# Three layer-norm statistics of every chunk, taken from VectorE and summed by ScalarE with its accumulator, in a Mamba block with a routed expert layer

## What is computed

```python
def _L0_attn_ref(x, ...):
    x = x + _mamba(_ln(x, n1_g, n1_b), ...)
    normed = _ln(x, n2_g, n2_b)
    gate, val = jnp.split(normed @ ffg_w.T + ffg_b, 2, axis=-1)
    return x + jax.nn.silu(gate) * val @ ffp_w.T + ffp_b
...
x = x + _L0_attn_ref(_layernorm(x, axis=-1), ...)   # the first norm, then _ln inside
x = x + _L0_ffn_ref(_layernorm(x, axis=-1), ...)    # top 2 of 8 experts, softmax weights
```

## Time and profile before

| | |
|---|---|
| runs | 896.98, 898.70, 903.21 us; median 898.7 us |
| the profiled execution | 898.42 us, of which the span of the engines is 896.5 us |
| VectorE | 726.3 us busy, 81% |
| TensorE | 666.5 us busy, 74% |
| GpSimd | 573.2 us busy, 64% |
| ScalarE | 504.6 us busy, 56% |
| scan phase | from about 45 us to 746 us |
| tail (expert tiles and the last chunk's output side) | 746 us to the end |

### The profile page before, as it was taken

How to read it: one execution, slowest core, us unless ns; L and a number is a source line. 1 busy time by engine, 2 the same in 40 slices (tenths; PEclk the granted TensorE clock), 3 DMA queues, 4 the chain that set the end, 5 groups by cost and what they waited for, 6 DMA issues and landing times. The chain is left out here.

```text
span 896.5 us, 13066 instructions
## 1 busy us (share of the span) xinstructions
PE 666.5 (74%) x3706; PEld 481.6 (54%) x3706; DVE 726.3 (81%) x1128; ACT 504.6 (56%) x1092; POOL 573.2 (64%) x488
## 2 busy tenths in 40 slices
PE   4358578678768886797788768877884877898963
PEld 2134245445335534774477446744673556798963
DVE  1378779989998999979998999999999865474363
ACT  2547676766766576556756575557553663443421
POOL 1095556566856895789768985888669934345332
PEclk9679699889879977998799988988797889999997
DMA  6833133213312336542654255434642423457794
GB/s 179 248 113 114 47 94 118 79 65 108 119 48 90 106 100 185 152 127 86 186 162 118 90 171 155 125 106 132 173 150 80 129 63 99 135 160 216 204 311 130
DMA packets 95450, 118.24 MB, mean 132 GB/s; under 512 B 11351, under 2 KB 63395, under 8 KB 95363
## 3 DMA queue, kind: packets, MB, share of 16 engines
q1 hardware_dynamic: 90835, 108.02, 41.3%
q0 software_dynamic: 4544, 9.38, 2.9%
HBM read 105.37 MB, written 16.34 MB: 136 GB/s over the span
## 5 line engine op out<-in xcount | busy, mean ns | idle before, releaser
L695 POOL TENSOR_TENSOR inflow<-du,b_wide 128x1024 f32<-128x1024 f32 x128 | 316.2, 2473 | 170.6 <-DVE product L960 109.4
L950 DVE TENSOR_TENSOR_SCAN state<-decay,carry,inflow 128x512 f32<-128x512 f32 x192 | 235.0, 1265 | 6.2 <-ACT decay L814 5.8
L814 ACT ACTIVATE decay<-delta,a_neg 128x512 f32<-128x512 f32 x256 | 171.9, 690 | 104.6 <-DVE state L950 101.1
L722 POOL DMA_INDIRECT y_dram<-y_rows,x_rows x78 | 86.8, 1112 | 82.0 <-ACT y_rows L870 73.4
L960 DVE TENSOR_TENSOR product<-state,c_wide 128x1024 f32<-128x1024 f32 (+1 forms) x98 | 135.8, 1386 | 2.8 <-PE y L1150 1.7
L1150 PE MATMUL y<-ident,product 128*128 128x128 f32 x704 | 106.2, 297 | 41.9 <-DVE product L960 41.8
L1150 PEld LDWEIGHTS y<-ident,product 128*128 128x128 f32 x704 | 87.2, 153 | 79.9 <-DVE product L960 50.0
L1155 PE MATMUL y<-h_rows,ident 128*128 128x512 f32 x160 | 101.2, 755 | 33.6 <-ACT h_rows L779 33.6
L716 POOL DMA_INDIRECT row_dram<-m_tok,place x64 | 72.7, 1136 | 25.8 <-issue 19.8
L950 DVE TENSOR_TENSOR_SCAN state<-decay,inflow 128x512 f32<-128x512 f32 x64 | 74.8, 1212 | 9.2 <-ACT decay L814 6.6
L1106 PE MATMUL work_front<-u_t,w_tap 128*128 128x512 f32 x128 | 64.1, 628 | 6.0 <-ACT u_t L750 4.4
(11 more groups left out here) (210 smaller groups left out, 1285.1 us busy)
## 6 DMA issues: line engine op xcount, KB each, us to landing
b_wide<-bc_dram SPq DMA_DIRECT2D x128, 256.0 KB, 3.3
w_stage<-gate_up_dram SPq DMA_DIRECT2D x78, 344.0 KB
c_wide<-bc_dram SPq DMA_DIRECT2D x98, 256.0 KB, 3.5
x_rows<-row_dram SPq DMA_DIRECT2D x78, 65.0 KB, 3.6
x_tok<-in_x SPq DMA_DIRECT2D x8, 256.0 KB, 6.2
out<-x_tok SPq DMA_DIRECT2D x8, 256.0 KB, 4.6
inflow<-y_dram SPq DMA_DIRECT2D x6, 256.0 KB, 4.2
gate_up_dram<-in_Wg SPq DMA_DIRECT2D x1, 1376.0 KB, 8.9
```

The lines of the kernel that those rows point to most:

```text
L695: e.tensor_tensor(inflow[:, key % 3], du[:, c % 2], b_wide[:, key % ROW_SLOTS:key % ROW_SLOTS + 1, :].to_broadcast([P, HALVES, CHUNK]), AL ...
L722: e.indirect_dma_start(y_dram, bass.IndirectOffsetOnAxis(x_rows[:, key % X_SLOTS, ID_AT:ROW].bitcast(u32), 0), y_rows[:, key % Y_SLOTS, :] ...
L814: e.activation(decay_bank[h][:], delta[:, c % 2, h, :], ACT.Exp, scale=a_neg[:, h, n:n + 1]).then_inc(S["decay"], 1)
L950: e.tensor_tensor_scan(state[:, key % STATE_SLOTS, h, :], decay_bank[h][:], inflow[:, key % 3, h, :], 0.0 if c % (SEQ // CHUNK) == 0 else ...
```

## The change

VectorE's `bn_stats`, `bn_aggr` and `shift` go, except for the very first norm (slot 0 of chunk 0, in front of everything). In their place ScalarE walks each chunk twice: `sums` copies each of the 4 tiles with scale -1/128 and lets the accumulator write the row sum, which is the negative mean; `squares` does Square with this mean as bias, and the accumulator writes the sum of squared distances. That is 8 instructions of 128x128 for each norm, for 7 + 8 + 8 = 23 norms. The elementwise results go to a scratch tile `summed` that nobody reads. GpSimd divides by 128 in the operation that adds EPS, and makes `shift` with one more multiplication behind rstd. Slot 0's sums and squares stand in `FRONT` row 0, slot 2's in `BACK` rows 3 and 4, slot 3's in row 10, ahead of and behind the scan.

```diff
 FRONT = [
-    ((), ("stats0",), ("z0",)),
+    ((), ("sums0", "squares0"), ("z0",)),
     (("rstd0", "rstd1", "tanh_z0"), ("silu0",), ("z1",)),
-    (("tanh_z1",), ("shift0", "silu1"), ("x_one",)),
+    (("tanh_z1",), ("silu1",), ("x_one",)),
     (("u_tok", "u_turn"), ("u_t", "halo"), ("in0a",)),
     ((), (), ("in0b",)),
     ((), ("conv0",), ("in1a",)),
@@ -83,15 +83,15 @@
     ((), ("y_gate",), ("y_turn0",)),
     ((), ("y_cols0",), ("y_turn1",)),
     ((), ("y_cols1",), ("out_proj",)),
-    ((), ("x_two", "stats2"), ()),
-    (("rstd2",), (), ()),
-    ((), ("shift2",), ("n_tok",)),
+    ((), ("x_two", "sums2"), ()),
+    (("squares2",), ("rstd2",), ()),
+    ((), (), ("n_tok",)),
     (("n_turn",), ("n_t",), ("ff_gate",)),
     ((), ("gate_h",), ("ff_val",)),
     ((), ("silu_g", "ff_h"), ("ff_out",)),
-    ((), ("x_four", "stats3"), ()),
-    (("rstd3",), (), ()),
-    ((), ("shift3",), ("m_tok",)),
+    ((), ("x_four",), ()),
+    (("sums3",), ("squares3", "rstd3"), ()),
+    ((), (), ("m_tok",)),
     (("m_turn",), ("m_t",), ("route_mm",)),
     ((), ("route", "top"), ("route_exp",)),
     ((), ("choice",), ("rank",)),
...
+        summed = sb("summed", [P, 2, SUB, D_MODEL])
         var_one = sb("var_one", [P, SUB])
-        stats = sb("stats", [P, 4, SUB, 6])
+        stats = sb("stats", [P, SUB, 6])
         mean_var = sb("mean_var", [P, 4, SUB, 2])
...
                 if name == "rstd0":
-                    e.wait_ge(S["aggr0"], SUB * (key + 1))
-                    if not key:
+                    if key:
+                        e.wait_ge(S["squares0"], SUB * key)
+                    else:
+                        e.wait_ge(S["aggr0"], SUB)
                         e.wait_ge(S["minus_half"], 1)
-                    e.tensor_scalar(rstd[:, 0, :], mean_var[:, 0, :, 1], EPS, None, ALU.add).then_inc(S["rstd0"], 1)
+                    e.tensor_scalar(rstd[:, 0, :], mean_var[:, 0, :, 1], 1.0 / D_MODEL if key else 1.0, EPS, ALU.mult, ALU.add).then_inc(S["rstd0"], 1)
                     e.wait_ge(S["rstd0"], 6 * key + 1)
                     e.tensor_tensor(rstd[:, 0, :], rstd[:, 0, :], minus_half[:], ALU.pow).then_inc(S["rstd0"], 1)
+                    if key:
+                        e.wait_ge(S["rstd0"], 6 * key + 2)
+                        e.tensor_tensor(shift[:, 0, :], mean_var[:, 0, :, 0], rstd[:, 0, :], ALU.mult).then_inc(S["shift0"], 1)
...
                 elif name == "rstd2":
-                    e.wait_ge(S["aggr2"], SUB * (key + 1))
-                    e.tensor_scalar(rstd[:, 2, :], mean_var[:, 2, :, 1], EPS, None, ALU.add).then_inc(S["rstd2"], 1)
+                    e.wait_ge(S["squares2"], SUB * (key + 1))
+                    e.tensor_scalar(rstd[:, 2, :], mean_var[:, 2, :, 1], 1.0 / D_MODEL, EPS, ALU.mult, ALU.add).then_inc(S["rstd2"], 1)
                     e.wait_ge(S["rstd2"], 2 * key + 1)
                     e.tensor_tensor(rstd[:, 2, :], rstd[:, 2, :], minus_half[:], ALU.pow).then_inc(S["rstd2"], 1)
+                    e.wait_ge(S["rstd2"], 2 * key + 2)
+                    e.tensor_tensor(shift[:, 2, :], mean_var[:, 2, :, 0], rstd[:, 2, :], ALU.mult).then_inc(S["shift2"], 1)
                 elif name == "rstd3":
...
+            def row_sums(slot, src, at):
+
+                if at:
+                    e.wait_ge(S[f"squares{slot}"], SUB * at)
+                for s in range(SUB):
+                    e.activation(summed[:, 0, s, :], src[:, s, :], ACT.Copy, scale=-1.0 / D_MODEL, accum_out=mean_var[:, slot, s, 0:1]).then_inc(S[f"sums{slot}"], 1)
+
+            def row_squares(slot, src, at):
+
+                e.wait_ge(S[f"sums{slot}"], SUB * (at + 1))
+                for s in range(SUB):
+                    e.activation(summed[:, 1, s, :], src[:, s, :], ACT.Square, bias=mean_var[:, slot, s, 0:1], accum_out=mean_var[:, slot, s, 1:2]).then_inc(S[f"squares{slot}"], 1)
+
             for name, key in order:
                 if name == "prepare":
                     e.wait_ge(S["d_front"], 16 * FRONT_LOADS)
                     e.activation(a_neg[:], a_neg[:], ACT.Exp).then_inc(S["a_exp"], 1)
+                elif name == "sums0":
+                    e.wait_ge(S[f"d_x{key}"], 16)
+                    e.wait_ge(S["rstd0"], 6 * key)
+                    e.wait_ge(S["shift0"], key)
+                    row_sums(0, x_tok[:, key], key - 1)
+                elif name == "squares0":
+                    row_squares(0, x_tok[:, key], key - 1)
+                elif name == "sums2":
+                    e.wait_ge(S["x_two"], key + 1)
+                    if key:
+                        e.wait_ge(S["shift2"], key)
+                    row_sums(2, x_two, key)
+                elif name == "squares2":
+                    row_squares(2, x_two, key)
+                elif name == "sums3":
+                    e.wait_ge(S["x_four"], key + 1)
+                    if key:
+                        e.wait_ge(S["shift3"], key)
+                    row_sums(3, x_tok[:, key], key)
+                elif name == "squares3":
+                    row_squares(3, x_tok[:, key], key)
...
-            def norm_stats(slot, src, c, landed):
-                e.wait_ge(*landed)
-                if c:
-                    e.wait_ge(S[f"aggr{slot}"], SUB * c)
-                for s in range(SUB):
-                    e.bn_stats(stats[:, slot, s, :], src[:, s, :]).then_inc(S[f"stats{slot}"], 1)
-                e.wait_ge(S[f"stats{slot}"], SUB * (c + 1))
-                for s in range(SUB):
-                    e.bn_aggr(mean_var[:, slot, s, :], stats[:, slot, s, :]).then_inc(S[f"aggr{slot}"], 1)
-
-            def norm_shift(slot):
-                e.scalar_tensor_tensor(shift[:, slot, :], mean_var[:, slot, :, 0], -1.0, rstd[:, slot, :], ALU.mult, ALU.mult).then_inc(S[f"shift{slot}"], 1)
-
...
                 elif name == "stats0":
-                    if key:
-                        e.wait_ge(S["u_tok"], SUB * key)
-                    norm_stats(0, x_tok[:, key], key, (S[f"d_x{key}"], 16))
+                    e.wait_ge(S["d_x0"], 16)
+                    for s in range(SUB):
+                        e.bn_stats(stats[:, s, :], x_tok[:, key, s, :]).then_inc(S["stats0"], 1)
+                    e.wait_ge(S["stats0"], SUB)
+                    for s in range(SUB):
+                        e.bn_aggr(mean_var[:, 0, s, :], stats[:, s, :]).then_inc(S["aggr0"], 1)
                 elif name == "shift0":
-                    e.wait_ge(S["rstd0"], 6 * key + 2)
-                    norm_shift(0)
+                    e.wait_ge(S["rstd0"], 2)
+                    e.scalar_tensor_tensor(shift[:, 0, :], mean_var[:, 0, :, 0], -1.0, rstd[:, 0, :], ALU.mult, ALU.mult).then_inc(S["shift0"], 1)
...
```

More of the change, by code:

```diff
@@ L461, in mamba_moe_block @@
             + ["halved", "a_exp", "a_neg", "diag", "minus_half", "ones", "ser_shift", "w_tap", "back_halved", "halo"]
-            + ["stats0", "aggr0", "stats2", "aggr2", "stats3", "aggr3", "rstd0", "rstd2", "rstd3", "shift0", "shift2", "shift3"]
+            + ["stats0", "aggr0", "sums0", "squares0", "sums2", "squares2", "sums3", "squares3", "rstd0", "rstd2", "rstd3", "shift0", "shift2", "shift3"]
             + ["x_one", "u_tok", "u_turn", "u_t", "in", "conv", "tanh_c", "xc", "x_proj", "x_dbl"]
@@ L672, in _ @@
                     e.wait_ge(S["rstd0"], 6 * key + 4)
-                    e.tensor_scalar(rstd[:, 1, :], var_one[:], EPS, None, ALU.add).then_inc(S["rstd0"], 1)
+                    e.tensor_scalar(rstd[:, 1, :], var_one[:], 1.0 / D_MODEL if key else 1.0, EPS, ALU.mult, ALU.add).then_inc(S["rstd0"], 1)
                     e.wait_ge(S["rstd0"], 6 * key + 5)
@@ L676, in _ @@
                 elif name == "rstd2":
-                    e.wait_ge(S["aggr2"], SUB * (key + 1))
-                    e.tensor_scalar(rstd[:, 2, :], mean_var[:, 2, :, 1], EPS, None, ALU.add).then_inc(S["rstd2"], 1)
+                    e.wait_ge(S["squares2"], SUB * (key + 1))
+                    e.tensor_scalar(rstd[:, 2, :], mean_var[:, 2, :, 1], 1.0 / D_MODEL, EPS, ALU.mult, ALU.add).then_inc(S["rstd2"], 1)
                     e.wait_ge(S["rstd2"], 2 * key + 1)
                     e.tensor_tensor(rstd[:, 2, :], rstd[:, 2, :], minus_half[:], ALU.pow).then_inc(S["rstd2"], 1)
+                    e.wait_ge(S["rstd2"], 2 * key + 2)
+                    e.tensor_tensor(shift[:, 2, :], mean_var[:, 2, :, 0], rstd[:, 2, :], ALU.mult).then_inc(S["shift2"], 1)
                 elif name == "rstd3":
-                    e.wait_ge(S["aggr3"], SUB * (key + 1))
-                    e.tensor_scalar(rstd[:, 3, :], mean_var[:, 3, :, 1], EPS, None, ALU.add).then_inc(S["rstd3"], 1)
+                    e.wait_ge(S["squares3"], SUB * (key + 1))
+                    e.tensor_scalar(rstd[:, 3, :], mean_var[:, 3, :, 1], 1.0 / D_MODEL, EPS, ALU.mult, ALU.add).then_inc(S["rstd3"], 1)
                     e.wait_ge(S["rstd3"], 2 * key + 1)
```

(12 more changed lines are left out.)

## The result

The changed kernel takes 903.2 us (median of 20 runs, 899.73 to 910.31) against 898.8 us before (20 runs beside them): ratio 1.0062, interval 1.0044 to 1.0081, some 5.6 us slower. The forecast was +11.3 us: the sign and the range hold, and the size is double what was measured. The profiled execution spans 900.3 us.

A forecast was written before the change was run, and what follows sets the result against it. VectorE led in busy share, but other engines take over inside a chunk, so costs were taken place by place: +9.9 - 3.9 + 2.1 + 0.6 + 2.6 = +11.3 us on 898.42, so 910 us; 8-in-10 range 884 to 922 us.

The forecast's parts named there:

- slot 0 without experts: Chunks 0 to 2, units 0 and 13: ScalarE's eight instructions delay `silu_z` and `decay` for VectorE's scan, +9.9 us together.
- slot 0 with experts: Chunks 3 to 5: the eight instructions fit in ScalarE's free time and VectorE keeps 3 x 1.3 us, -3.9 us.
- slot 2, tail too: Units 3 to 5, seven chunks: no gain, GpSimd's extra multiplication costs +2.1 us; last chunk's tail partly hidden, +0.4 us.
- slot 3, tail too: Units 9 to 12, seven chunks: small wins and port losses, +0.6 us; in the tail, longer statistics lengthen the chain 2.2 us.
- Gain: none: Slot 2, units 3 to 5: VectorE coming 1.3 us sooner waits 1.3 us longer for the same `inflow`, set by GpSimd's queue.
- count `shift` at nothing: VectorE's `shift`, 17.2 us for 24 norms: removing it wins nothing, as the hold falls on `xc` or `product`.
- ScalarE's price: Eight instructions for a norm take 3.5 us on ScalarE, bounded by 2.0 and 4.2 us; 80 us more for 23 norms.
- The rival that VectorE is the bound and all is won: Whole kernel: what leaves VectorE is won if held `product` and `shift` are freed, about 883 us; chance 0.25.
- The cancel rival: Whole kernel: ScalarE's price is 2.0 us or slot 2 yields half its 1.3 us, 898 to 906 us; chance 0.25.

The follow-up runs named there:

- the last experiments: Changed kernel rewritten with the experiments' table (1.0030); best version with slot 2's offset on VectorE (0.9934), or with its statistics there and offset on GpSimd (0.9969).
- r16: Control: the changed kernel written with the table all experiments share, same instructions in the same order; ratio 1.0030 to the kernel before.
- r5: The changed kernel with slot 2's offset alone back on VectorE, its statistics still on ScalarE; ratio 1.0113 to the kernel before.
- r18: r9 with slot 2's statistics on VectorE, the offset on GpSimd directly ahead of the inflow of unit 7; ratio 0.9969 to the kernel before.
- r9: Best version: the changed kernel with only slot 0 of chunks 5 to 7 and slot 2 of chunks 0 to 6 on ScalarE; 893.05 us, ratio 0.9920.

## Right and wrong, by the prediction's steps

| term | forecast, us | against 1.0062, us | against 1.0030, us |
|---|---|---|---|
| slot 0 without experts | +9.9 | +9.5 | +6.7 |
| slot 0 with experts | -3.9 | -5.6 | -8.4 |
| slot 2, tail too | +2.1 + 0.4 | -4.7 | -7.5 |
| slot 3, tail too | +0.6 + 2.2 | +4.2 | +1.3 |
| whole change | +11.3 | +5.6 | +2.7 |

Each figure is a difference of ratios by 898.8 us. Against 1.0062 the terms sum to +3.4 us where the whole is +5.6; against 1.0030 they sum to -7.9 where it is +2.7, since the base's own uncertainty is in each of the four. Besides, the slots act on one another, as the last experiments show.

- **The step that failed** is slot 2: "Gain: none", and in the first part "count `shift` at nothing". Slot 2 with its tail was put at +2.5 us; it is -4.7, a difference of 7 us, the whole error and more. The reasoning held that VectorE, 1.3 us sooner, would wait 1.3 us longer for the same `inflow`, whose start GpSimd's own queue sets. In the trace that start moves: `inflow` of unit 7 (the prediction called it unit 6's) begins at 29.5 us in the changed kernel and at 27.8 in r16, against 28.9 before, and `xc` ends 3.0 and 1.2 us sooner than before. By the runs the statistics yield 4.4 us over seven norms in the best version, half of the 1.3 us each, and the place of the offset and of `rstd2` yields 4.6 to 8 us beside slot 3 on ScalarE and nothing measurable without it. In chunk 5 of the changed kernel `xc` takes 1.20 and `product` 0.68 us, where the prediction looked for "over 2 us"; in r16 `xc` takes its 2.64. How the 4.7 us split between the statistics, the hold and the order of the queue stays open.
- **`shift` counted at nothing** has the sum of busy time for it: VectorE's fell by 22.3 us, less even than the 30 to 35 forecast. The time has not: with the offset alone back on VectorE (r5) 4.6 us are lost. Busy time didn't tell the gain, since a kernel in which VectorE is held at another place has the same sum. In chunks 6 and 7 r5 also makes VectorE wait, 6.3 us in sum, for an `rstd2` that comes late from ScalarE's squares, so its loss is not the hold's alone.
- **ScalarE's price** was within its bounds and too high: the eight instructions at unit 13 of chunk 0 take 118.73 to 121.59 us, 2.86 us, for a forecast of 3.5. The read-out is a row of its own, as taken, but it overlaps. Slot 0 without experts came out at its forecast all the same (9.5 for 9.9), in part by luck: the price was lower, and the waits in chunks 1 and 2 were longer. In chunk 0 the waits are where they were put. At unit 0 of chunk 0 (forecast +2.6 us) and at unit 13 (1.99 us before in the earlier trace rows), VectorE:

```profile
53.44 0.69 DVE L972 SCALAR_TENSOR_TENSOR silu_z<-silu_z,work_front 128x512 f32<-128x512 f32 x1 [2.95 <-ACT silu_z L849]
...
122.20 0.69 DVE L972 SCALAR_TENSOR_TENSOR silu_z<-silu_z,work_front 128x512 f32<-128x512 f32 x1 [4.81 <-ACT silu_z L849]
```

In unit 13 of chunks 1 and 2 the wait is another one than the forecast's. It priced `decay` (+2.4 and +1.4 us) and named `route_exp` of chunk 2 without a price; VectorE waits for just that, `top_w` from ScalarE behind the eight. Before, it waited 0 and 0.40 us for it. The changed kernel:

```profile
205.31 0.18 DVE L1050 TENSOR_SCALAR top_w<-top_w 128x4 f32<-128x4 f32 x1 [3.94 <-ACT top_w L899]
...
289.98 0.18 DVE L1050 TENSOR_SCALAR top_w<-top_w 128x4 f32<-128x4 f32 x1 [4.14 <-ACT top_w L899]
```

- **Slot 0 with experts**: right in sign, 5.6 us for 3.9.
- **Slot 3**: the tail's 2.2 us is 2.5 in the trace, and slot 2's 0.4 is 0. That `rstd3` gets late was foreseen (53.0 to 56.8 us in chunk 6); what it costs by itself is small (2.2 us in seven chunks, not told from nothing), but it took away the slack that other delays need.
- **The rival that VectorE is the bound and all is won** fell in its size: 883 us is not reached by any version. Its condition, "the held `product` and `shift` are no longer held", was met in some chunks only, and the start that it hung on ("which nothing in the change does") did move: in chunk 5 by +0.6 us in the changed kernel and by -1.1 in r16. The Trainium skill (Perfetto Trace Analysis, Optimizing Scalar/DVE Operations) says that offloading from a saturated VectorE may make sense; the runs agree for ten of the norms (0.9920 with these moved) and differ where ScalarE's queue feeds a scan (9.5 us lost on four norms). **The cancel rival**, 898 to 906 us, gave the time. Its second cause, slot 2 yielding half of its 1.3 us in seven chunks (-4.6 us), is what r18 against r9 measures (4.4 us); of its first, a price of 2.0 us, less than half came true (2.86).

## What to carry over

Work moved off a busy engine should be moved place by place: here four of 23 norms cost more than the other nineteen won in sum, and a version with ten of them on the other engine is 0.8% faster than before while all 23 are 0.6% slower. When two engines hold each other, list what the change puts directly ahead of the long instruction in the other engine's queue, since that can move its start, and look at it in every chunk and in a second execution before calling it the cause; and before counting a delay, ask which queue further on has slack to take it up, because one more dependence between in-order engines can remove that slack.
